# The hyperbolic attention loop takes its two square-root forms in another order of units

## The reference, cut to what matters

```
qk = einsum('bhnd,bhmd->bhnm', q, k)
diff_sq  = maximum(q_norm_sq + k_norm_sq - 2.0 * qk, 0.0)
denom    = maximum((1.0 - q_norm_sq) * (1.0 - k_norm_sq), 1e-06)
cosh_arg = maximum(1.0 + 2.0 * diff_sq / denom, 1.0)
distance = where(cosh_arg > 1.0, arccosh(cosh_arg), 0.0)
attn = softmax(-distance, axis=-1)
out  = einsum('bhnm,bhmd->bhnd', attn, v)
```

## Time and profile before

| | us |
|---|---|
| median of 3 runs | 1403.53 (1402.94 to 1404.54) |
| the profiled execution | 1396.75 |
| its span, first to last instruction | 1395.0 |

### The profile page before, as it was taken

How to read it: one execution, slowest core, us unless ns; L and a number is a source line. 1 busy time by engine, 2 the same in 40 slices (tenths; PEclk the granted TensorE clock), 3 DMA queues, 4 the chain that set the end, 5 groups by cost and what they waited for, 6 DMA issues and landing times. The chain is left out here.

```text
span 1395.0 us, 17991 instructions
## 1 busy us (share of the span) xinstructions
PE 990.5 (71%) x5593; PEld 494.9 (35%) x5593; DVE 960.9 (69%) x2063; ACT 747.0 (54%) x858; POOL 495.9 (36%) x298
## 2 busy tenths in 40 slices
PE   5877723489999737999254678778889889354394
PEld 2553222256666436998120001111111112024393
DVE  6666697367777263554647999999999999336511
ACT  4204513225555613443141599999999999941041
POOL 0000000200000005663043787778776887200074
PEclk9998955669999857999575555665555555665597
DMA  4001000212110015664224200010000100020164
GB/s 142 0 1 27 1 0 19 70 46 84 40 34 23 9 31 188 209 213 130 70 77 110 75 29 23 23 39 29 23 23 32 36 23 0 0 63 5 46 185 121
DMA packets 67732, 80.17 MB, mean 57 GB/s; under 512 B 13185, under 2 KB 46780, under 8 KB 67648
## 3 DMA queue, kind: packets, MB, share of 16 engines
q1 hardware_dynamic: 59520, 68.90, 16.1%
q0 software_dynamic: 3968, 8.13, 1.9%
q10 hardware_dynamic: 4160, 2.10, 0.5%
HBM read 63.56 MB, written 15.34 MB: 57 GB/s over the span
## 5 line engine op out<-in xcount | busy, mean ns | idle before, releaser
L2503 POOL TENSOR_TENSOR hb_t<-hb_t,hb_r 128x1024 f32<-128x1024 f32 x124 | 329.9, 2698 | 106.5 <-ACT hb_r L2312 106.5
L2515 DVE TENSOR_SCALAR hb_dpos<-hb_psR 128x1024 f32<-128x1024 f32 x128 | 155.6, 1217 | 31.2 <-PE hb_psR L2240 26.2
L2249 PE MATMUL hb_psR<-ha_q,ha_k 20*128 20x512 bf16 x256 | 127.7, 598 | 55.3 <-DVE hb_dpos L2515 55.0
L2523 DVE SCALAR_TENSOR_TENSOR hb_t<-hb_psR,hb_dpos 128x1024 f32<-128x1024 f32 x128 | 155.1, 1212 | 0.0
L2261 PE MATMUL hb_psO<-hb_t,ha_va 128*9 128x512 f32 x512 | 115.4, 1002 | 50.3 <-ACT hb_t L2335 50.3
L2240 PE MATMUL hb_psR<-ha_q,ha_k 78*128 78x512 bf16 x256 | 128.4, 604 | 26.2 <-DMA ha_k<-hsx 20.1
L1865 DVE TENSOR_REDUCE ga_nm<-ga_psA 128x1 f32<-128x128 f32 (+3 forms) x256 | 112.9, 484 | 46.9 <-PE ga_psA L1751 46.8
L1844 ACT ACTIVATE ga_att<-ga_psB 128x1024 f32<-128x1024 f32 (+3 forms) x128 | 86.9, 709 | 99.8 <-PE ga_psB L1776 99.8
L2532 DVE SCALAR_TENSOR_TENSOR hb_r<-hb_t 128x1024 f32<-128x1024 f32 x64 | 125.8, 1966 | 0.0
L2335 ACT ACTIVATE hb_t<-hb_t 128x4096 f32<-128x4096 f32 x32 | 113.8, 3602 | 0.0
L1619 POOL MEMSET ga_q<- 64x8192 bf16 x1 | 6.9, 6919 | 249.5 <-POOLq L1546 249.5
(11 more groups left out here) (459 smaller groups left out, 2195.9 us busy)
## 6 DMA issues: line engine op xcount, KB each, us to landing
m2x_e_w<-in_L_ffn_W_dram SPq DMA_DIRECT2D x78, 256.0 KB
m1x_e_w<-in_L_ffn_W_dram SPq DMA_DIRECT2D x23, 256.0 KB
ga_q<-qx SPq DMA_DIRECT2D x48, 96.0 KB
ha_q<-hqx SPq DMA_DIRECT2D x48, 96.0 KB
ha_k<-hkx SPq DMA_DIRECT2D x16, 288.0 KB
hy_fwd<-in_const_fwd_dram SPq DMA_DIRECT2D x1, 2048.0 KB
f_down<-in_L_ffn_W_dram ACTq DMA_DIRECT2D x4, 512.0 KB, 3.9
m2x_c_got<-m2x_outputs SPq DMA_DIRECT2D x8, 256.0 KB
```

The source lines that it names most:

```text
L2249: mm = pe.matmul(psR[:, side_slot(n), i, :], k[SIDE:SIDE + SROWS, it % 2, i0 + i, P * c:P * c + P], q[SIDE:SIDE + SROWS, it % 2, i0 + i, : ...
L2503: pool.tensor_tensor(tt, tt, r[:, (2 * it + form) % R_QUADS, k, :], ALU.add).then_inc(sum_ready, 1)
L2515: dve.tensor_scalar(dpos[:, n % 2, :], psR[:, dist_slot(n), :, :].rearrange("p i t -> p (i t)"), 0.0, None, ALU.max).then_inc(dpos_ready, 1)
L2523: dve.scalar_tensor_tensor(out=unit(t, n), in0=psR[:, side_slot(n), :, :].rearrange("p i t -> p (i t)"), scalar=CAP, in1=dpos[:, n % 2, :] ...
```

## The change

Units 0 to 3 of a step become the form of the two roots (form 1) and units 4 to 7 the product form (form 0). `values` reads each chunk from where it now lies and waits for the Exp of its form: chunks 0 and 1 for form 1, chunks 2 and 3 for form 0. The wait of `ratio` for a free slot is rewritten to the same chunk of the unit as before.

```diff
             def place(n):
                 it, p = n // UNITS, (n % UNITS) // 2
-                return it, p % 2, 2 * (p // 2) + n % 2
+                return it, 1 - p // 2, 2 * (p % 2) + n % 2
...
                     def values(it, c):
-                        pe.wait_ge(w_ready, 2 * it + c % 2 + 1)
+                        pe.wait_ge(w_ready, 2 * it + (1 - c // 2) + 1)
...
-                                           t[:, (2 * it + c % 2) % T_QUADS, 2 * (c // 2) + i // 2, SEQ * (i % 2):SEQ * (i % 2) + SEQ],
+                                           t[:, (2 * it + 1 - c // 2) % T_QUADS, 2 * (c % 2) + i // 2, SEQ * (i % 2):SEQ * (i % 2) + SEQ],
...
                         if it >= 3:
-                            dve.wait_ge(used, CH * (it - 3) + 2 * (k // 2) + form + 1)
+                            dve.wait_ge(used, CH * (it - 3) + (n % UNITS) // 2 + 1)
```

## The result

The changed kernel takes **1540.3 us** (1535.8 to 1541.1) against 1404.0 us in the same comparison, a ratio of 1.096 with a 95% interval of 1.094 to 1.099. Its profiled execution has a span of 1534.0 us, 139.0 more than before. Forecast were 1540 us for the median and about 1534 for the profiled execution, which took 1535.8.

A forecast was written before the change was run, and what follows sets the result against it. ScalarE was taken to bound the kernel, with VectorE hardly ahead of it. The intervals' +132, the start's +3 and the tail's +2 gave +137 us, so a median of about 1540 us, range 1523 to 1552.

The forecast's parts named there:

- the chain: From the second Exp's end through `values`, `turn_out`, `distances`, clips, ratios and products to the next root: 11.15 us.
- the 14 intervals: Root-to-root intervals from the second step to the last: 524.4 us in place of 392.4, so +132.0.
- The ring and its length: ScalarE's next root waits for a product behind its own second Exp, so work adds: 37.42 us a step against 27.58.
- VectorE's wait ahead of the chain: Sign in the profile: at position 7 VectorE waits for TensorE's L2240 or `turn_out`, 6 to 7 us.
- The clock: TensorE runs at its low clock in each step after some 6 us idle: 37.42 us, against 36.90 if fast.
- The start: Second step's roots wait for step 1's last product, two positions later: +3 us, bounds 0 and 5.
- one collision with GpSimd fewer: Before the second step's roots, one of two products meeting GpSimd should remain, giving back about 1.4 us.
- The tail: After the last step, `values` of chunk 0 and `turn_out` come behind the second Exp: +2 us, bounds 1.4 and 2.7.
- Only the later Exp counts: Rival: no ring closes, each step comes 3.5 us later: 49 plus 5, 1458 us; chance 0.05.
- VectorE gets ahead: Rival: at most one of four products in a row collides, VectorE outruns ScalarE: 1403.6 or 1398.6 us; chance 0.04.

The follow-up runs named there:

- e2: Kernel before the change with only the products two positions later, `values` of chunk 0 still waiting for the first Exp: 1484.0 us, ratio 1.058.
- e5: Changed kernel with ScalarE's two Exps in the other order, `values` of chunks 0 and 1 waiting for the first of them: 1487.2 us, ratio 1.059.
- e6: Changed kernel with product(n - 1) in place of product(n - 2), so the last product stands behind one clip instead of two: 1486.9 us, ratio 1.058.
- e4: Changed kernel with `values` of chunk 1 also at position 7, behind chunk 0, so more TensorE work follows the Exp: 1546.5 us, ratio 1.102.
- e1: Kernel before the change with only the wait of `values` for chunk 0 moved to the second Exp, order of units and products unchanged: 1418.0 us, ratio 1.011.
- e3: Changed kernel with `values` of chunks 0 and 1 moved back to position 2 of the step after: 1455.2 us, ratio 1.037.
- e7: Changed kernel with product(n - 1) and `values` of chunks 0 and 1 behind the `distances` of position 0: 1435.0 us, ratio 1.021.
- e8: As e7, with the Exp of form 1 first and chunks 0 and 1 waiting for that one alone: 1424.1 us, ratio 1.014.

## Why the prediction was right

It was right in mechanism and in size: the chain's 11.15 us and the step's 37.42 were met to a hundredth. That the total came within 2 us (+137 forecast, +139.0 measured in the profile, +136.3 in the medians) is partly luck, since its terms were off by +3.0 (start), -4.4 (the 14 intervals), +0.6 (tail) and 2.7 that were not foreseen. Step by step:

- *The ring and its length.* Forecast were 26.27 + 11.15 = 37.42 us a step; 37.43 in most steps. That the products close it and the Exp sets its length is shown by e2 and e5, its length through VectorE by e6. The sum over 14 intervals was to be 524.4 us; it was 520.0 (801.16 to 1321.20), so +127.6 and not +132.0. 3.6 of these 4.4 us I missed by my own reading of the order: behind the last step there are no more units, so positions 0 and 1 have no clips, and the last interval, which holds the third copy of a batch, is 34.27 long and not 37.9. The other 0.8 are the second and third of the 14, 36.97 and 37.06 long. VectorE's wait ahead of the chain is 9.48 us and not the 6 to 7 that were named as a sign, since it lasts through `values` and `turn_out` behind the Exp.
- *The clock.* Low level, 0.51 of full in the stretch. Taking 37.42 and not 36.90 was right. TensorE's idle time ahead of the chain was 12.77 us in most steps, though, twice the 6 of the prediction. e4 shows how near the other level is: with sixteen matmuls on end it was reached by the end of `distances` in 10 of 12 steps.
- *The start.* Forecast +3, measured +6.0 (795.13 to 801.16), and +6.9 when counted from the loop's first clip, which stands 0.9 us earlier in this execution (740.77 against 741.67). The two positions are as counted; the term that failed is the 1.4 us that one collision with GpSimd fewer was to give back. VectorE before the second step's roots, beside the earlier trace rows:

```profile
784.47 2.09 DVE L2532 SCALAR_TENSOR_TENSOR hb_r<-hb_t 128x1024 f32<-128x1024 f32 x1
...
788.74 3.40 DVE L2532 SCALAR_TENSOR_TENSOR hb_r<-hb_t 128x1024 f32<-128x1024 f32 x1
...
794.33 3.40 DVE L2532 SCALAR_TENSOR_TENSOR hb_r<-hb_t 128x1024 f32<-128x1024 f32 x1
```

Three products in a row met it, and lost 5.3 us where two had lost 3.0. That is not the change's doing alone: in e1, with VectorE's old order, three met it as well at this place.

- *The tail.* Forecast +2; from the last step's roots to the last addition of the loop it is 53.8 us (1321.20 to 1374.97) against 51.1, so +2.6. `values` of chunk 0 and `turn_out` came behind the last Exp, as said.
- *The rest.* Behind the loop, 2.7 us of the 139.0 appeared in stages that the change does not touch. Their cause was not looked for and stays open.
- 6.0 + 127.6 + 2.6 + 2.7 = 138.9. The errors of the start and of the last interval nearly cancel, which is luck.
- *The rivals.* "Only the later Exp counts" is what e1 shows of that wait alone, and even there it is 16 us and not 49. "VectorE gets ahead" rested on at most one collision a step, and in 11 of the 14 intervals of the changed kernel there is just one: its products lose 2.0 us a step to GpSimd, against 3.2 before. The gain is there and is worth nothing behind the ring, as the prediction said. Whether VectorE would get ahead in exactly this order without a ring is not shown: e3 has this order but a ring through the buffer, and e7 and e8 have each product a turn earlier, where two or three collide in each step.

## What to carry to other kernels

When an instruction waits on an in-order engine, list what stands behind it and follow that until it reaches the engine it waits for: if it closes within one step, work that overlapped is added up, and the price is nearly the whole chain in every step, here 11.15 us less the 1.3 that a table load fills, however small the shift was. Two edits can be small or moderate apart and cost more together than their sum (16 and 82 us against 136), so cost them as a pair. And when such a ring is opened, look for the next one: here one ran through the buffers, whose slots come back behind the same wait, and one through an engine that another one had to wait for.

## What the runs showed of the hardware

- A product whose input is the result of the instruction right before it starts 1.24 us after that one (994.81 to 996.05 in e8), with another instruction between them it is 1.13: 0.11 us on VectorE for 128 x 1024 float32.
- A product (two SBUF inputs) that starts while one of GpSimd's additions of 2.37 us has more than 0.1 us left ends 1.08 or 1.09 us after the addition, in all 336 such cases of the 12 traces: its time is what the addition has left plus 1.09, up to 3.35. In 122 cases it started with 0.06 us or less left; it took 1.21 in 99 of them and 3.40 to 3.45 in the other 23, when it waited for the next addition as well. The second product of a pair stands at this edge in the old order, so 0.11 us more put it behind the edge: 3.31 to 3.33 in every step of e8.
- More work on TensorE in a waiting chain made the matmuls behind it faster: in the changed kernel 8 matmuls of `values` and a `turn_out` were followed by `distances` at 1.06 us in 11 of 12 steps, in e4 16 of them by `distances` at 0.60 to 0.82 in 10 of 12.
